# First image's coefficient sums and reconstruction ahead of the odd set's correlation on TensorE

## The chip, the cores and the metric

The kernel runs on one core of one Trainium2 chip. The metric is the device time of one execution in microseconds, the median over several runs. Three runs of the kernel before gave 530.71, 532.79 and 532.80 us.

## What is computed

x is 16 images of 32 channels by 64 by 64, in float32. Each image is normalised per channel, goes through a 3x3 convolution with ternary weights (two weight sets, merged by a gate), and is added to x. The result x1 is normalised again (z) and cut into 256 patches per image, of 32 channels x 4 x 4 = 512 values. Each patch is written by orthogonal matching pursuit as a sum of 5 of 256 normalised dictionary columns, and the sum is added to x1. Cut to what matters:

```python
D = dictionary / (norm(dictionary, axis=0) + 1e-10)       # 512 x 256
G = D.T @ D + 1e-5 * eye(256)
h_bar = (D.T @ X).T                                       # the correlation
h = h_bar
for k in range(1, 6):
    index = argmax(abs(h * ~mask), axis=1)
    ...                                                   # one more row of a Cholesky factor, new x_stack
    h = h_bar - einsum('bk,bkn->bn', x_stack, G[I])
coeffs = zeros((B, 256)).at[bidx[:, None], I].set(x_stack)
X_hat = D @ coeffs.T
x = x + conv(gn(x));  x = x + patches_back(X_hat(gn(x)))
```

## The kernel before, in words

The images are taken in four rounds r = 0 to 3 of four images. A round's patches are two sets: set 0 (the even one) is images 0 and 1 of the round, set 1 (the odd one) images 2 and 3; each set has four tiles of 128 patches. For each set PSUM holds the scores h, one 128x256 block per tile.

Each engine has its order written out by hand; semaphores tie the orders together. `body(r, front, behind)` is one round on one engine. With `front` it also prepares the next round f = r + 1 (statistics of x, convolution, normalisation to z); with `behind` it also finishes images of the round before, b = r - 1. Round 0 has no `behind`, round 3 no `front`.

Matching pursuit (VectorE): per step k and set, `scan` (L992 maxima of |h|, L1005 or L1007 their indices), `select` (the new index; L1049 lets GpSimd gather the Gram rows), `extract` (L1062 picks), `solve` (small solves, whose steps stand between those of the other set's scan). `all_picked(s)` (L983) says at the end of a set's last extraction that h of the set may be overwritten (semaphore `h_read`). In the last step of set 1, `spread(r, 0)` (L1199, L1203) writes four of five terms of image 0's coefficients: five of its eight instructions stand in `select`, the last three after `all_picked(1)`, and then L1208 raises `coef_ready`. ScalarE makes the fifth term (L703, `make_terms`) at the end of the round.

TensorE: `correlate(f, 0)` ends a round's body, `correlate(r, 1)` begins the next; each is 16 products, 32 instructions in the profile (a float32 product shows as two). `correlate(r, 1)` waits for `h_read` of set 1. `coef_transposes(b, m)` transposes and sums the coefficient terms of image m into PSUM: 8 instructions on ScalarE's term, then a wait for `coef_ready`, then 8 on VectorE's. ScalarE's `copy_coef(b, m)` (L689) brings the sum to SBUF, and `reconstruct(b, m)` multiplies it with the atoms (16 instructions). ScalarE's `out_back` (L714) copies the result out; the next image's `coef_transposes` waits for that.

ScalarE, around the start of a round: `scores(f, 0, 0)` for set 0 at the end of the body before; then `x_statistics` of four images (L623), `scores(r, 1, 0)` (L674), `copy_coef(b, 0)`, `root`, `diags(r, 0, 0)` (L683), `out_back(b, 0)`, `norm_x(f, 0)` (L640), `scores(r, 0, 1)`, `copy_coef(b, 1)`, `make_terms` of two images, `norm_x(f, 1)`, `diags(r, 1, 0)`. TensorE's `x_sums(f)` adds the statistics over the channels, VectorE's `variance` (L921 to L935) stands in the scan of set 1, then `root` on ScalarE, then `norm_params` (L941 to L957) on VectorE after the `select` of set 1; it raises `x_params`, for which `norm_x(f, 0)` waits. All matrix products are issued from L391.

Of the kernel before, what the change touches and what calls it, by code (L numbers as in the profile page):

```python
# [32 lines left out]
def build_program(nc, x_in, w_in, b_in, wc_in, bc_in, gate_in, dict_in, out):  # L33
# [25 lines left out]
    with ctx:  # L59
# [81 lines left out]
        def terms_of(r, m):  # L141

            if r < ROUNDS - 1:
                return coef[:, (m + 2) % IMG_R, :, :].rearrange("p (i t) n -> p i t n", i=1)
            first = 2 * ATOMS * sum(ACT_TERMS[r][:m])
            part = spare_z[:, first:first + 2 * ATOMS * ACT_TERMS[r][m]]
            return part.rearrange("p (i t n) -> p i t n", t=2, n=ATOMS)
# [241 lines left out]
        def _(pe):  # L389
            def mm(dst, lhs, rhs, start, stop, skip=False):  # L390
                return nc.tensor.matmul(dst, lhs, rhs, start=start, stop=stop, skip_group_check=skip)  # L391
# [4 lines left out]
            def x_sums(f):  # L396
                pe.wait_ge(x_stats, 2 * IMG_R * (f + 1))
                mm(conv_ps[:, 0, 0:2 * IMG_R], same_channel[:, :], sum_x[:, :, :].rearrange("p a m -> p (a m)"),
                   True, True).then_inc(x_stats_ps, 1)
# [51 lines left out]
            def correlate(f, s):  # L451

                if not (isinstance(f, int) and f == 0):
                    pe.wait_ge(h_read[s], STEPS * f)
                for t in range(TILES):
                    if t % 2 == 0:
                        pe.wait_ge(z_done, IMG_R * f + 2 * s + t // 2 + 1)
                    zt = z[:, 2 * s + t // 2, t % 2 * HALF:(t % 2 + 1) * HALF].rearrange("p (n c) -> p c n", c=PATCH)
                    for c in range(PATCH):
                        last = mm(h[s][:, t, :], zt[:, c, :], d_sb[:, c, :], t % 2 == 0 and c == 0, c == PATCH - 1, True)  # L460
                    if t % 2:
                        last.then_inc(h_ready[s], 1)
# [16 lines left out]
            def coef_transposes(r, m, dst=back_ps[0]):  # L479

                n = IMG_R * r + m
                pe.wait_ge(terms_ready, n + 1)
                if dst is back_ps[0]:
                    pe.wait_ge(y_done, 2 * n + 2)
                of_act = terms_of(r, m)
                for i in range(ACT_TERMS[r][m] + 1):
                    if i == ACT_TERMS[r][m]:
                        pe.wait_ge(coef_ready, n + 1)
                    for k in range(CHUNKS):
                        for t in range(2):  # L490
                            part = coef[:, m, t, :] if i == ACT_TERMS[r][m] else of_act[:, i, t, :]
                            last = mm(dst[:, k, t * P:(t + 1) * P], part[:, k * P:(k + 1) * P], ident[:, :],
                                      i == 0 and k == 0 and t == 0, i == ACT_TERMS[r][m], True)
                last.then_inc(coef_t_ps, 1)
# [10 lines left out]
            def reconstruct(r, m):  # L505

                for half in (1, 0):
                    add_atoms(IMG_R * r + m, half, back_ps[half])
# [30 lines left out]
            def body(r, front, behind):  # L539
                f = r + 1  # L540
                b = r - 1
                idle_bank = conv_ps[:, 1, 0:ATOMS] if behind else back_ps[1][:, 0, :]
                correlate(r, 1)
                if front:
                    x_sums(f)
                if behind:
                    coef_transposes(b, 0)
                    reconstruct(b, 0)
                update(r, 0, 0)
                if behind:  # L550
                    coef_transposes(b, 1)
                    reconstruct(b, 1)
                update(r, 1, 0)
                if not front:
                    pe.wait_ge(x1_done, 2 * IMG_R * ROUNDS)
                if front:
                    conv(f, 0)
                else:
                    keep_busy(idle_bank, 8)
                update(r, 0, 1)  # L560
                if front:
                    conv(f, 1)
                else:
                    keep_busy(idle_bank, 8)
                update(r, 1, 1)
                if front:
                    conv(f, 2)
                else:
                    keep_busy(idle_bank, 8)
                update(r, 0, 2)  # L570
                if front:
                    conv(f, 3)
                else:
                    keep_busy(idle_bank, 6)
                if behind:
                    coef_transposes(b, 2)
                update(r, 1, 2)
                if behind:
                    reconstruct(b, 2)
                else:  # L580
                    keep_busy(idle_bank, 7)
                if front:
                    y_sums(f)
                update(r, 0, 3)
                if behind:
                    coef_transposes(b, 3)
                    reconstruct(b, 3)
                else:
                    keep_busy(idle_bank, 8)
                update(r, 1, 3)  # L590
                if front:
                    correlate(f, 0)
# [9 lines left out]
        def _(act):  # L602
# [83 lines left out]
            def copy_coef(r, m, src=back_ps[0], dst=coef_t):  # L686
                n = IMG_R * r + m
                act.wait_ge(coef_t_ps, n + 1)
                nc.scalar.activation(dst[:, :, :], src[:, :, :], ACT.Copy, scale=-1.0).then_inc(coef_t_done, 1)  # L689
# [62 lines left out]
            def body(r, front, behind):  # L752
                f = r + 1
                b = r - 1
                if front and behind:
                    for m in range(IMG_R):
                        x_statistics(f, m)
                scores(r, 1, 0)
                if behind:
                    copy_coef(b, 0)  # L760
                if front:
                    root(x_var, x_root, 0, f)
                diags(r, 0, 0)
                if behind:
                    out_back(b, 0)
                if front:
                    norm_x(f, 0)
                scores(r, 0, 1)
                if behind:
                    copy_coef(b, 1)  # L770
                    make_terms(b, 2)
                    make_terms(b, 3)
                if front:
                    norm_x(f, 1)
                diags(r, 1, 0)
                if behind:
                    out_back(b, 1)
                scores(r, 1, 1)
                if front:
                    norm_x(f, 2)  # L780
                diags(r, 0, 1)
                if front:
                    out_conv(f, 0)
                scores(r, 0, 2)
                if front:
                    norm_x(f, 3)
                diags(r, 1, 1)
                if front:
                    out_conv(f, 1)
                scores(r, 1, 2)  # L790
                if front:
                    square_sum(f, 0)
                diags(r, 0, 2)
                if front:
                    out_conv(f, 2)
                scores(r, 0, 3)
                if front:
                    square_sum(f, 1)
                diags(r, 1, 2)
                if front:  # L800
                    out_conv(f, 3)
                if behind:
                    copy_coef(b, 2)
                scores(r, 1, 3)
                if front:
                    square_sum(f, 2)
                    square_sum(f, 3)
                diags(r, 0, 3)
                if behind:
                    out_back(b, 2)  # L810
                if front:
                    root(y_var, y_root, 1, f)
                scores(r, 0, 4)
                if behind:
                    copy_coef(b, 3)
                diags(r, 1, 3)
                if front:
                    norm_y(f, 0)
                    norm_y(f, 1)
                if behind:  # L820
                    out_back(b, 3)
                scores(r, 1, 4)
                if front:
                    norm_y(f, 2)
                    norm_y(f, 3)
                    make_terms(r, 0)
                    make_terms(r, 1)
                    scores(f, 0, 0)
# [567 lines left out]
```

## Time and profile before

| | us |
|---|---|
| median of the runs | 532.79 |
| lowest, highest | 530.71, 532.80 |
| the profiled execution, its own time | 535.74 |
| its span, first to last instruction | 533.7 |
| TensorE busy | 429.4 (80%) |
| VectorE busy | 447.4 (84%) |
| ScalarE busy | 317.7 (60%) |
| mean granted TensorE clock | 0.942 of full |

PE is TensorE, PEld its weight loads, DVE VectorE, ACT ScalarE, POOL GpSimd; a q behind the name (DVEq) is the engine's sequencer, which raises semaphores. In a timeline a row gives the start, the time to the end of the last instruction in it, the engine, the line, the operation, the output and the inputs, the count, and in brackets the idle time before with what ended it. Busy time of overlapping instructions is not additive.

### The profile page before, as it was taken

The page shows a single profiled execution, that of the slowest core. Times are in us where ns is not written, and L with a number is a line of the kernel's source. Part 1 is how long each engine was busy: PE and PEld are TensorE (multiplying, and loading weights), DVE is VectorE, ACT ScalarE, POOL GpSimd, SP SyncE. Part 2 cuts the span into 40 slices and gives each one's busy share as a digit, 9 for nine tenths or more (in the row PEclk, how much of TensorE's full clock was granted, in tenths as well). Part 3 has the DMA queues.
Part 4 walks back from the last instruction along what each step waited for, and adds up shares of the span by engine and source line. Part 5 has one row for each costly group of instructions (what it writes and reads, how often), then busy time and mean ns, then how long its engine had stood idle before and what let it go on. Part 6 is the DMA issues. An engine that isn't in the chain of part 4 may idle for free.

```text
span 533.7 us, 7983 instructions
## 1 busy us (share of the span) xinstructions
PE 429.4 (80%) x1948; PEld 324.7 (61%) x1948; DVE 447.4 (84%) x2268; ACT 317.7 (60%) x712; POOL 147.5 (28%) x162
## 2 busy tenths in 40 slices
PE   0089974999885869999894979999958897988685
PEld 0033862556665755557774864568757776867574
DVE  4665668888899959978999889998999999989983
ACT  2535448856558359866697299757740754456340
POOL 3000044433300153532300355443000764430010
PEclk9999997999889887999997899999997999989798
DMA  5999712899300043999510174521400665224256
GB/s 99 176 143 151 139 40 72 139 168 147 68 1 1 9 101 89 161 177 174 119 41 1 29 168 112 132 64 47 83 1 1 158 153 133 68 67 88 47 109 128
DMA packets 110206, 50.76 MB, mean 95 GB/s; under 512 B 103632, under 2 KB 104144, under 8 KB 110160
## 3 DMA queue, kind: packets, MB, share of 16 engines
q1 hardware_dynamic: 99480, 25.60, 29.8%
q0 software_dynamic: 8160, 24.13, 19.6%
q10 hardware_dynamic: 2520, 0.53, 0.5%
q8 instruction: 16, 0.26, 0.2%
q14 instruction: 30, 0.25, 0.2%
HBM read 34.24 MB, written 8.65 MB: 80 GB/s over the span
## 4 chain that ended last, share of the span: by engine, by line
PE 50%; DVE 29%; ACT 8%; issue 6%; SPq 3%; another core or an unknown queue 1%; DMA 1%; DVEq 0%; ACTq 0%
PE h L391 30%; PE conv_ps L391 15%; DVE junk L1062 9%; PE back_ps L391 6%; DVE top L992 3%; SPq L261 3%; DVE top_i L1007 2%; DVE top_i L1005 2%; ACT diag L683 2%; ACT score L674 2%; DVE coef L1203 2%; DVE mask L1089 2%; ACT xb L640 1%; ACT xa L640 1%
## 5 line engine op out<-in xcount | busy, mean ns | idle before, releaser
L363 POOL DMA_INDIRECT rows<-gram,idx_u x128 | 129.1, 1009 | 329.3 <-DVEq L1049 299.2
L391 PE MATMUL h<-rows,diag 128*128 128x256 f32 x640 | 152.3, 395 | 26.0 <-ACT diag L683 22.0
L391 PEld LDWEIGHTS h<-rows,diag 128*128 128x128 f32 x640 | 123.9, 197 | 54.9 <-issue 37.5
L1062 DVE SCALAR_TENSOR_TENSOR junk<-mask,rows 128x256 bf16<-128x256 bf16 x320 | 119.1, 417 | 0.0
L683 ACT ACTIVATE diag<-ident,dx 128x128 f32<-128x128 f32 x320 | 96.8, 388 | 34.8 <-DVEq L1156 33.0
L674 ACT ACTIVATE score<-h 128x512 f32<-128x512 f32 x80 | 47.0, 596 | 97.4 <-PE h L391 85.6
L992 DVE MAX8 top<-score 128x8 f32<-128x256 f32 x160 | 65.1, 418 | 34.5 <-ACT score L674 30.4
L391 PE MATMUL h<-d_sb,z 128*128 128x256 f32 x256 | 68.2, 431 | 23.7 <-DVEq L983 23.7
L391 PEld LDWEIGHTS h<-d_sb,z 128*128 128x128 f32 x256 | 63.5, 329 | 28.7 <-DVEq L983 25.4
L391 PE MATMUL conv_ps<-xa,w_taps 128*64 128x512 f32 x128 | 62.6, 612 | 4.0 <-DVEq L1267 4.0
L391 PE MATMUL conv_ps<-xb,w_taps 128*64 128x512 f32 x128 | 62.6, 612 | 0.0
L391 PE MATMUL back_ps<-coef_t,d_t 128*128 128x256 f32 x224 | 54.1, 397 | 8.9 <-ACT coef_t L689 8.2
L391 PEld LDWEIGHTS back_ps<-coef_t,d_t 128*128 128x128 f32 x224 | 43.3, 197 | 16.9 <-ACT coef_t L689 8.2
L1005 DVE FIND_INDEX8 top_i<-top,h 128x8 uint32<-128x256 f32 x128 | 52.1, 423 | 0.0
L1203 DVE SCALAR_TENSOR_TENSOR coef<-mask,x_last,coef 128x256 f32<-128x256 bf16 x92 | 40.3, 476 | 0.0
L714 ACT ACTIVATE y<-back_ps 128x512 f32<-128x512 f32 x28 | 29.2, 1110 | 11.8 <-PE back_ps L391 7.8
L391 PEld LDWEIGHTS conv_ps<-xa,w_taps 128*64 128x64 f32 x128 | 16.5, 138 | 31.2 <-issue 27.1
L391 PE MATMUL conv_ps<-xa,w_mid 128*64 128x512 f32 x64 | 32.8, 593 | 0.0
L391 PE MATMUL conv_ps<-xb,w_mid 128*64 128x512 f32 x64 | 32.7, 592 | 0.0
L1089 DVE TENSOR_SCALAR mask<-iota_short,idx_u 128x256 bf16<-128x256 bf16 x128 | 28.7, 286 | 3.6 <-DVE idx_u L1044 0.5
L623 ACT ACTIVATE z<-xa 128x1088 bf16<-128x1088 f32 x23 | 25.2, 1099 | 9.5 <-DMA xa<-in_x 9.5
L652 ACT ACTIVATE x<-conv_ps,gn 128x512 f32<-128x512 f32 x32 | 21.5, 674 | 13.7 <-PE conv_ps L391 13.7
(156 smaller groups left out, 569.2 us busy)
## 6 DMA issues: line engine op xcount, KB each, us to landing
xa<-in_x SPq DMA_DIRECT2D x64, 128.0 KB
out<-x SPq DMA_DIRECT2D x60, 128.0 KB, 2.7
x<-y POOLq DMA_DIRECT2D x14, 512.0 KB
xb<-in_x SPq DMA_DIRECT2D x48, 128.0 KB, 4.9
rows<-gram,idx_u POOLq DMA_INDIRECT x128
xb<-in_x SPq DMA_DIRECT2D x16, 120.0 KB, 5.3
d_sb<-in_L_conv_dictionary SPq DMA_DIRECT2D x4, 128.0 KB, 3.9
out<-x ACTq DMA_DIRECT2D x4, 128.0 KB
```

The costliest lines, as they stand in the source:

```text
L363: pool.indirect_dma_start(out=rows[s][:, k, t, :], out_offset=None, in_=gram_dram[:, :], in_offset=bass.IndirectOffsetOnAxis(ap=idx_u[s][: ...
L391: return nc.tensor.matmul(dst, lhs, rhs, start=start, stop=stop, skip_group_check=skip)
L623: nc.scalar.activation(unread[:, n % 3], xa[:, m, :, 1:W + 1], func, accum_out=sum_x[:, i, m:m + 1]).then_inc(x_stats, 1)
L652: nc.scalar.activation(image_of(x1, n)[:, b * HALF:(b + 1) * HALF], conv_ps[:, b, :], ACT.Identity, bias=gn[:, 0, 10, m:m + 1], accum_out= ...
L674: nc.scalar.activation(score[s][:, 2 * b:2 * b + 2, :], h[s][:, 2 * b:2 * b + 2, :], ACT.Abs).then_inc(score_ready[s], 1)
L683: last = nc.scalar.activation(diag[s][:, t, j, :], ident[:, :], ACT.Copy, scale=dx[s][:, k, t, j:j + 1])
L714: nc.scalar.activation(dst[:, 2 * half:2 * half + 2, :], src[half][:, :, :], ACT.Copy).then_inc(y_done, 1)
L992: c = step(v.max(out=top[s][:, t, 0:16:2], in_=score[s][:, t, :]))
L1005: step(v.max_index(out=top_i[s][:, t, :], in_max=top[s][:, t, 0:8], in_values=h[s][:, t, :]))
L1062: c = step(v.scalar_tensor_tensor(out=place, in0=mask_of(r, s, k, t), scalar=1.0, in1=source, op0=ALU.mult, op1=ALU.mult, accum_out=dst))
L1089: marked.append(step(v.tensor_scalar(mask_of(r, s, k, t), iota_short[:, :], idx_u[s][:, k, t:t + 1], None, ALU.is_equal)))
L1203: added.append(step(v.scalar_tensor_tensor(out=coef[:, m, t, :], in0=mask_of(r, s, j, tile), scalar=x, in1=coef[:, m, t, :], op0=ALU.mult, ...
```

## The change

Two moves, in every round that has `behind` (1, 2 and 3). On TensorE the transposes and the reconstruction of image 0 of the round before now stand ahead of `correlate(r, 1)` and `x_sums(f)`, not behind them. On ScalarE the copy between these two products now stands ahead of the statistics of x and of the odd set's scores. No instruction is added or taken away.

```diff
@@ -540,12 +540,12 @@        (block.tensor, body)
                 idle_bank = conv_ps[:, 1, 0:ATOMS] if behind else back_ps[1][:, 0, :]
-                correlate(r, 1)
-                if front:
-                    x_sums(f)
                 if behind:
                     coef_transposes(b, 0)
                     reconstruct(b, 0)
+                correlate(r, 1)
+                if front:
+                    x_sums(f)
                 update(r, 0, 0)
@@ -752,12 +752,12 @@        (block.scalar, body)
+                if behind:
+                    copy_coef(b, 0)
                 if front and behind:
                     for m in range(IMG_R):
                         x_statistics(f, m)
                 scores(r, 1, 0)
-                if behind:
-                    copy_coef(b, 0)
                 if front:
                     root(x_var, x_root, 0, f)
```

## Rows read from the trace of the kernel before

**Rows 1.** The page: the engines' shares of the chain that ended last.

```profile
PE 50%; DVE 29%; ACT 8%; issue 6%; SPq 3%; another core or an unknown queue 1%; DMA 1%; DVEq 0%; ACTq 0%
```

**Rows 2.** Chain of waits, start of round 2 and its middle: start us, us, what.

```profile
291.82 0.03 DVEq L983
...
291.90 10.51 PE h L391 x32
...
302.53 1.90 PE back_ps L391 x16
...
304.45 0.61 ACT coef_t L689
...
305.10 3.73 PE back_ps L391 x16
...
318.94 1.97 PE h L391 x8
...
361.99 0.61 ACT score L674
```

**Rows 3.** Waits of the whole span: engine, line, releaser, total us, times, longest.

```profile
PE h L391 <- DVEq L983: 23.7, 5, 7.4
```

**Rows 4.** Timeline of VectorE, start of round 2: last of image 0's coefficient instructions.

```profile
293.03 0.45 DVE L1203 SCALAR_TENSOR_TENSOR coef<-mask,x_last,coef 128x256 f32<-128x256 bf16 x1
```

**Rows 5.** Timeline of TensorE: `correlate(1, 0)`, at full clock.

```profile
159.97 7.63 PE L391 MATMUL h<-d_sb,z 128*128 128x256 f32 x32
```

**Rows 6.** Granted clock by windows: window, length, busy of five engines, PEclk, DMA.

```profile
168.00:175.00 7.00, 0.01 (x1) 0.01 (x1) 6.88 (x42) 7.00 (x14) 0.00 (x0) 0.77 0.00 0
...
288.00:292.00 4.00, 0.10 (x1) 0.10 (x1) 3.85 (x25) 4.00 (x9) 0.00 (x0) 0.50 0.00 0
...
296.00:299.00 3.00, 3.00 (x11) 2.56 (x10) 2.75 (x8) 0.28 (x1) 0.00 (x0) 0.65 0.00 0
...
312.00:314.00 2.00, 0.33 (x3) 0.14 (x2) 0.85 (x5) 2.00 (x6) 1.70 (x3) 1.00 0.60 140
```

**Rows 7.** Timeline of TensorE, round 1: second image's transposes and reconstruction, at half clock.

```profile
196.64 3.75 PE L391 MATMUL back_ps<-ident,coef 128*128 128x128 f32 x16 [3.51 <-ACT y L714]
201.08 6.11 PE L391 MATMUL back_ps<-coef_t,d_t 128*128 128x256 f32 x16 [0.69 <-ACT coef_t L689]
```

**Rows 8.** Timeline of ScalarE, start of round 2: last statistics, normalisation, diagonals.

```profile
293.06 1.09 ACT L623 ACTIVATE z<-xa 128x1088 bf16<-128x1088 f32 x1
...
309.76 1.15 ACT L640 ACTIVATE xa<-xa,gn 128x960 f32<-128x960 f32 x1
...
318.39 1.28 ACT L683 ACTIVATE diag<-ident,dx 128x128 f32<-128x128 f32 x4
```

**Rows 9.** Timeline of VectorE, round 2: odd set's scan, variance, parameters.

```profile
301.39 0.43 DVE L992 MAX8 top<-score 128x8 f32<-128x256 f32 x1
...
304.22 0.20 DVE L935 TENSOR_SCALAR gn<-gn 128x4 f32<-128x4 f32 x1
...
309.07 0.15 DVE L957 SCALAR_TENSOR_TENSOR gn<-gn 128x4 f32<-128x4 f32 x1
```

**Rows 10.** Timeline of ScalarE, round 1: first image's copy out, then the normalisation.

```profile
190.36 1.13 ACT L714 ACTIVATE y<-back_ps 128x512 f32<-128x512 f32 x1 [2.12 <-PE back_ps L391]
195.43 1.07 ACT L714 ACTIVATE y<-back_ps 128x512 f32<-128x512 f32 x1 [3.94 <-remote]
196.29 1.15 ACT L640 ACTIVATE xa<-xa,gn 128x960 f32<-128x960 f32 x1
```

**Rows 11.** Timeline of TensorE, then VectorE, start of round 3.

```profile
402.76 9.77 PE L391 MATMUL h<-d_sb,z 128*128 128x256 f32 x32 [7.02 <-DVEq L983]
...
416.96 2.46 DVE L1203 SCALAR_TENSOR_TENSOR coef<-mask,x_last,coef 128x256 f32<-128x256 bf16 x6
420.32 0.43 DVE L992 MAX8 top<-score 128x8 f32<-128x256 f32 x1 [0.90 <-ACT score L674]
```

**Rows 12.** Chain of waits in round 3: its last VectorE piece of that stretch.

```profile
448.09 0.47 DVE top_i L1005 x2
```

More of the change, by code:

```diff
@@ L542, in body @@
                 idle_bank = conv_ps[:, 1, 0:ATOMS] if behind else back_ps[1][:, 0, :]
+                if behind:
+                    coef_transposes(b, 0)
+                    reconstruct(b, 0)
                 correlate(r, 1)
@@ L545, in body @@
                     x_sums(f)
-                if behind:
-                    coef_transposes(b, 0)
-                    reconstruct(b, 0)
                 update(r, 0, 0)
@@ L754, in body @@
                 b = r - 1
+                if behind:
+                    copy_coef(b, 0)
                 if front and behind:
@@ L758, in body @@
                 scores(r, 1, 0)
-                if behind:
-                    copy_coef(b, 0)
                 if front:
```

## The prediction

> **What bounds the kernel now.** I read the page's chain first: half of it is TensorE and 29% VectorE [rows 1], so neither engine alone is the bound; they hand the work to each other. Then the chain in order of time at the three round starts with something behind them, where the diff acts. Round 2 is typical [rows 2]: VectorE's last extraction of set 1 releases h at 291.85, TensorE runs `correlate(2, 1)` from 291.90, the sums of x, the transposes, the copy (0.61) and the reconstruction to 308.83. From 318.94 to 361.99 the chain's pieces (nine, two of them shown) are TensorE's without a gap, so what is late at 318.94 stays late. Third, the waits: TensorE stood idle 23.7 us over five waits for L983, up to 7.4 each [rows 3]. That is the hole into which the change puts work. The question is whether that work is ready while the hole is open.
>
> **Is the moved work ready?** The transposes need ScalarE's term and VectorE's four. The latter are complete only when L1208 raises `coef_ready`, and in program order three of the eight instructions of `spread` come after the release of h. In the trace the last of them runs 293.03 to 293.48 [rows 4]; `coef_ready` comes at about 293.5, that is 1.65 us after the release at 291.85 [rows 2]. So only the first 8 of 16 transposing instructions can use the hole; half of 1.90 us, 0.95. The rest starts when h has been free for 1.65 us already, and `correlate(r, 1)` now stands behind it.
>
> **TensorE, start of `correlate(r, 1)`.** New delay against the release of h: 1.65 (wait for `coef_ready`) + 0.95 (second half of the transposes, half of 1.90) + 0.67 (the copy with its two hand-overs, from 304.43 to 305.10) + 3.73 (reconstruction), all from [rows 2, 4]: 7.0 us. The copy in the middle can start at once, since ScalarE is idle there once the statistics are put behind it.
>
> **The clock.** The granted clock falls to half in the hole (0.77 over 168 to 175, 0.50 over 288 to 292) and is back at full only some way into the work (0.65 over 296 to 299) [rows 6]. `correlate(1, 0)` at full clock took 7.63 us [rows 5]; `correlate(r, 1)` took 10.51 in round 2 [rows 2] and 9.77 in round 3 [rows 11], so the cold start costs 2.9 and 2.1 (1.7 in round 1, where it took 9.4 by the same view). After the change the cold start falls on the transposes, a wait for the copy and the reconstruction. The nearest rows are those of round 1 after another idle stretch: 3.75 and 6.11 us [rows 7] where 1.90 and 3.73 are normal, a cost of 4.2 for the whole, or 0.9 + 2.4 = 3.3 for the part that would count here. The first 8 transposes may keep the clock up, and the cost could be nothing. I take 3.2, which is 1.0 more than the mean of before (2.2), with bounds of 2.2 less and 2.0 more.
>
> In a sentence by itself: the Trainium skill, page TensorE: Matmul & The Clock Gate, section What's actually happening, says that the default state is throttled and that activity releases it; by that rule work put into the hole would shorten the cold part, and the sum would be lower by up to 2.2 per round. The trace has the half clock in this hole, but no row with 1 us of work in the middle of it.
>
> **What follows from x_sums (rounds 1 and 2).** Let X be the end of `x_sums`, 302.53 in round 2. It moves by 7.0 + 1.0 = 8.0. Behind X: the variance on VectorE is over at 304.42 (X + 1.9) and the last step of the parameters at 309.22 (X + 6.7) [rows 9], with the odd set's scan and `select` between them, which also trail `correlate(r, 1)`. `norm_x(2+1, 0)` began at 309.76, X + 7.2, since the copy out of image 0 had to end first [rows 8]; then come `scores(2, 0, 1)`, the second image's copy, `norm_x` of the next image and `diags(2, 1, 0)` at 318.39, and TensorE's `update` at 318.94 [rows 2, 8]. After the change the reconstruction is long done, so the copy out follows the diagonals at once and ends about X + 5.5 (variance 1.9, diagonals 1.28 [rows 8], two copies of 1.13 [rows 10]): `x_params` is last, at about X + 6.8. It gains 0.4 on before. Round 2 therefore ends 8.0 - 0.4 = 7.6 later.
>
> New holes also open on TensorE: behind X nothing is left until `diags(r, 0, 0)`, some 3 us, and again about 3.8 us between the second image's transposes (X + 5.5 to 7.5) and its copy (X + 11.3). In round 2 of before the clock stayed up through a shorter hole (1.00 over 312 to 314, with 0.33 of work) [rows 6]. A fall like that of [rows 7] would cost 2.4 on the reconstruction and some on the convolution. 0 to 4; I take 1.0.
>
> **Round 1** has a peculiarity: the second copy out waited 3.94 us for nothing that the profile can name, and `norm_x` began at 196.29, or X + 11.8 (X = 184.5) [rows 10]. Part of that stall becomes cover. If the stall stays at that instruction, the copies are at X + 3.3 and X + 8.3, `norm_x` at X + 9.2: a gain of 2.6 on before, and a bit more since [rows 7] came out cold behind it (reconstruction end X + 22.7 before, about X + 19 after: up to 3.5). If the stall disappears, 5.0. I take 3.3: 8.0 - 3.3 = 4.7.
>
> **Round 3** has no x to prepare. VectorE ended its `spread` at 419.42 and waited 0.90 for the scores of the even set [rows 11]. The odd set's scan and the `spread` behind it trail `correlate(3, 1)`; the even set's scores are now ready in their shadow. VectorE is the late one: 8.0 - 0.9 = 7.1. From there VectorE carries most of the chain, up to 448.56 [rows 12], so it stays.
>
> **ScalarE's move.** Before, the eight statistics (1.09 each) ended at 294.15 [rows 8], within the wait for `correlate`. Now they wait for the copy, to about 295.2, and take 8.9 us, to 304.1. The odd set's first scores come at about 305 and `x_sums` at about 310, so this costs nothing; the cover is 1 us for the scores and 6 for the sums. Without it, the statistics would delay the odd set's scan one for one. SyncE's and GpSimd's orders are untouched; the gather of the odd set's rows starts 8 us later but its last row is due only at X + 16, and the gather itself begins near X + 3.7 and needs about 7: no cost.
>
> **The sum.** 4.7 + 7.6 + 1.0 + 7.1 = 20.4 us. The profiled execution took 535.74 with a span of 533.7; it would take 556.1. The median of before is 532.79, which gives 553.2 us; I say 553.
>
> **Rivals.** (a) Slower as above, for all three rounds: 0.80. Its own range: per round 5.8 to 10 for X instead of 8.0. Low end: round 1 5.8 - 5.0 = 0.8, round 2 5.4, round 3 4.9, sum 11. High end: 10 - 2.6, 9.6 + 4, 9.1, sum 30. Both ends at once in all rounds are unlikely; 543 to 562.
> (b) The clock stays up because the array works in the hole: the term of 3.2 falls to 0 to 1. Then X moves by 7.0 - 2.2 = 4.8 to 5.8, and the total is 1.5 + 4.4 + 3.9 = 10 to 13, or 543 to 546. For it: the hole is cut by 1 us of work. Against: the clock had fallen in both holes of [rows 6] after work that was dense to their start, and 7 us of idle are still left. Chance 0.11.
> (c) Hidden: `correlate(r, 1)` isn't what ends last. VectorE began the odd set's scan at 301.39 [rows 9] without a wait and met X only 1 us later, so that set has about 1 us of slack, not 8; the chain would have to recover 7 us somewhere. 531 to 536, chance 0.04.
> (d) Faster, the other side: the wait for the copy out of image 0 ahead of `norm_x` is what matters, as the chain of round 2 names it, and the work of the block (1.90 + 0.7 + 3.73 = 6.3) leaves the path into the hole of 7. That needs `coef_ready` 6.3 - 1.65, some 4.7 us or more, before the release of h; it decides at the point where `coef_ready` precedes the release. Then up to 6.3 per round are gained, 19 in all: 514. The trace has it 1.65 behind the release [rows 2, 4], and the order of VectorE isn't changed. Chance 0.02.
> (e) Slower by more than (a): the unnamed stall of ScalarE or the cold convolution comes up in more rounds, 4 us each: 562 to 570, chance 0.03.
>
> **How the numbers follow.** The time is that of (a), 553. The range of 543 to 562 takes in (a) but its extremes, and (b). By 0.5% (2.7 us, about what a measurement of this kernel can tell from no change): faster 0.02, the same 0.04, slower 0.94.
>
> **What the profile of the changed kernel would show.** Right: in each of rounds 1 to 3, 8 transposes right behind `correlate(f, 0)`, an idle stretch that now ends with L1208 and not with L983, a reconstruction, and `correlate(r, 1)` beginning about 7 to 9 us after the release of h; the odd set's scan waiting for scores on VectorE for some 8 us; the copy out no longer ahead of `norm_x` in the chain, `x_params` in its place. Wrong: if `correlate(r, 1)` starts late and the first `update` of set 1 doesn't, I misread what is last; if it starts less than 6 us late, the clock term is wrong; if the hole ends before L983, the reading of `coef_ready` is.

## The result: the changed kernel is slower

The changed kernel takes 553.45 us (median; 551.40 to 557.56) beside 531.75 us for the kernel before in the same runs: a ratio of 1.0425, interval 1.0349 to 1.0501. The forecast was 553.0 us, 543 to 562, slower. Ratios, here and below, leave out runs that were slower than the others at a lower clock, so a ratio can differ a little from that of two medians.

The profiled execution took 554.57 us, its span is 552.6 (533.7 before). TensorE's busy time went from 429.4 to 437.8 us and its mean granted clock from 0.942 to 0.925. The page of the changed kernel, part 1 and the chain by engine (to set beside the table and [rows 1]):

```profile
PE 437.8 (79%) x1948; PEld 331.6 (60%) x1948; DVE 447.6 (81%) x2268; ACT 317.0 (57%) x712; POOL 146.7 (27%) x162
...
PE 45%; DVE 34%; ACT 9%; issue 6%; SPq 3%; another core or an unknown queue 1%; DMA 1%; DVEq 0%; ACTq 0%
```

The waits of the changed kernel, whole span, as in [rows 3]:

```profile
DVE top L992 <- ACT score L674: 45.0, 26, 6.1
...
PE back_ps L391 <- DVEq L1208: 23.7, 3, 8.1
...
PE h L391 <- DVEq L983: 2.3, 2, 1.2
```

The hole is still there, three times up to 8.1 us. It now ends with `coef_ready` (L1208), not with the release of h (L983). VectorE waits 45.0 us for scores (L992); in the kernel before:

```profile
DVE top L992 <- ACT score L674: 30.4, 22, 6.4
```

The chain of waits at the start of round 2, changed kernel (start us, us, what), beside [rows 2]:

```profile
295.80 0.02 DVEq L983
...
297.10 0.37 DVE coef L1203
...
297.58 2.09 PE back_ps L391 x8
...
299.69 0.61 ACT coef_t L689
...
300.34 6.68 PE back_ps L391 x16
307.02 7.48 PE h L391 x32
...
314.52 0.61 ACT score L674
...
317.14 3.39 PE h L391 x8
...
325.86 5.41 PE back_ps L391 x16
331.27 1.73 PE h L391 x8
```

h is free at 295.82 and `correlate(2, 1)` begins at 307.02, 11.2 us later; in the kernel before it began 0.05 us after the release. 1.76 us pass until the transposes go on, 2.09 + 0.67 + 6.68 us are the second half of the transposes, the copy and the reconstruction, and all of it is on the chain. Here is the clock in this stretch (window, its length, busy of five engines, PEclk, DMA), as in [rows 6]:

```profile
289.00:297.00 8.00, 0.75 (x7) 0.56 (x6) 7.85 (x45) 0.50 (x1) 0.00 (x0) 0.73 0.00 0
297.00:303.00 6.00, 4.74 (x14) 3.97 (x15) 5.50 (x18) 3.31 (x6) 0.00 (x0) 0.50 0.00 0
303.00:307.00 4.00, 4.00 (x12) 3.24 (x11) 2.18 (x12) 4.00 (x9) 1.16 (x2) 0.58 0.00 0
```

The transposes in the hole did not hold the clock; the reconstruction runs at half of it (1.2 GHz) for the most part, and `correlate` gets the full one (7.48 us).

ScalarE and VectorE behind it, round 2 of the changed kernel, timelines (to set beside [rows 8] and [rows 9]):

```profile
314.64 0.17 DVE L921 TENSOR_SCALAR gn<-conv_ps 128x8 f32<-128x8 f32 x1 [2.39 <-PE conv_ps L391]
...
321.19 0.15 DVE L957 SCALAR_TENSOR_TENSOR gn<-gn 128x4 f32<-128x4 f32 x1
```

```profile
307.83 1.10 ACT L623 ACTIVATE z<-xa 128x1088 bf16<-128x1088 f32 x1
...
317.78 1.98 ACT L714 ACTIVATE y<-back_ps 128x512 f32<-128x512 f32 x2
321.44 1.19 ACT L640 ACTIVATE xa<-xa,gn 128x960 f32<-128x960 f32 x1 [1.68 <-DVEq L961]
```

`norm_x` now waits 1.68 us for L961, which raises `x_params`; the copy out (L714) was over before. The statistics end at 308.93 and `x_sums` comes at 314.3: their cover held.

How much each round costs can be read from one marker, the step L1183 of the odd set's last solve, right behind the release of h. The timelines of VectorE, kernel before, then changed kernel:

```profile
175.03 0.24 DVE L1183 TENSOR_REDUCE n_inv<-prod 128x20 f32<-128x80 f32 x1
...
291.93 0.24 DVE L1183 TENSOR_REDUCE n_inv<-prod 128x20 f32<-128x80 f32 x1
...
402.80 0.24 DVE L1183 TENSOR_REDUCE n_inv<-prod 128x20 f32<-128x80 f32 x1
```

```profile
176.77 0.24 DVE L1183 TENSOR_REDUCE n_inv<-prod 128x20 f32<-128x80 f32 x1
...
295.91 0.24 DVE L1183 TENSOR_REDUCE n_inv<-prod 128x20 f32<-128x80 f32 x1
...
414.89 0.23 DVE L1183 TENSOR_REDUCE n_inv<-prod 128x20 f32<-128x80 f32 x1
```

| | before | changed | difference |
|---|---|---|---|
| up to round 1 (nothing changed) | 175.03 | 176.77 | 1.7 |
| round 1 | 116.90 | 119.14 | 2.2 |
| round 2 | 110.87 | 118.98 | 8.1 |
| round 3 and the end of the span | 130.90 | 137.71 | 6.8 |

The 1.7 us of round 0 is no effect of the change, since nothing differs there. ScalarE has stalls of some 3 us with no releaser that the profile knows (marked "remote"), up to three of them in a profile, and they fall differently from one profile to the next. The changed kernel's had two of them in round 0:

```profile
102.02 0.60 ACT L674 ACTIVATE score<-h 128x512 f32<-128x512 f32 x1 [2.88 <-remote]
...
123.12 0.60 ACT L674 ACTIVATE score<-h 128x512 f32<-128x512 f32 x1 [3.11 <-remote]
```

That of the kernel before had one there. In three later profiles without any in that stretch (half_ahead_2, only_r1, only_r2), where round 0 is the same, the marker stands at 171.10 to 171.86.

### The profile page after: what moved, and what is told of

The parts are those of the page before. It is cut to its first block, busy times and chain, and to the rows that moved or that the text cites. A ratio compares the mean times of both kernels' runs of the same rounds, so it can differ in the third digit from the quotient of the medians.

```text
span 552.6 us, 7983 instructions
## 1 busy us (share of the span) xinstructions
PE 437.8 (79%) x1948; PEld 331.6 (60%) x1948; DVE 447.6 (81%) x2268; ACT 317.0 (57%) x712; POOL 146.7 (27%) x162
## 3 DMA queue, kind: packets, MB, share of 16 engines
q0 software_dynamic: 8160, 24.13, 18.6%
## 4 chain that ended last, share of the span: by engine, by line
PE 45%; DVE 34%; ACT 9%; issue 6%; SPq 3%; another core or an unknown queue 1%; DMA 1%; DVEq 0%; ACTq 0%
PE h L391 25%; PE conv_ps L391 13%; DVE junk L1062 9%; PE back_ps L391 7%; DVE top L992 4%; DVE top_i L1005 3%; DVE coef L1203 3%; SPq L261 3%; ACT diag L683 2%; DVE top_i L1007 2%; ACT score L674 2%; DVE mask L1089 2%; ACT xb L640 2%; DVE coef L1199 1%
## 5 line engine op out<-in xcount | busy, mean ns | idle before, releaser
L391 PE MATMUL h<-rows,diag 128*128 128x256 f32 x640 | 156.9, 404 | 34.4 <-ACT diag L683 29.6
L391 PEld LDWEIGHTS h<-rows,diag 128*128 128x128 f32 x640 | 126.9, 202 | 64.5 <-issue 46.5
L992 DVE MAX8 top<-score 128x8 f32<-128x256 f32 x160 | 65.1, 418 | 47.1 <-ACT score L674 45.0
L391 PE MATMUL back_ps<-coef_t,d_t 128*128 128x256 f32 x224 | 60.7, 432 | 11.6 <-ACT coef_t L689 10.8
L391 PE MATMUL h<-d_sb,z 128*128 128x256 f32 x256 | 61.6, 400 | 2.3 <-DVEq L983 2.3
L391 PEld LDWEIGHTS h<-d_sb,z 128*128 128x128 f32 x256 | 60.3, 328 | 3.7 <-DVEq L983 3.1
L391 PEld LDWEIGHTS back_ps<-coef_t,d_t 128*128 128x128 f32 x224 | 48.0, 219 | 21.8 <-ACT coef_t L689 11.1
L391 PE MATMUL back_ps<-ident,coef 128*128 128x128 f32 x192 | 28.4, 306 | 24.5 <-DVEq L1208 23.7
L391 PEld LDWEIGHTS back_ps<-ident,coef 128*128 128x128 f32 x192 | 27.2, 218 | 27.6 <-DVEq L1208 24.3
```

The source lines that it names most:

```text
L992: c = step(v.max(out=top[s][:, t, 0:16:2], in_=score[s][:, t, :]))
```

## The experiments

All times are medians; a ratio is against runs of the kernel before on the same chip.

**1. Only the transposes ahead (recon_behind).** Against the changed kernel:

```diff
                 if behind:
                     coef_transposes(b, 0)
-                    reconstruct(b, 0)
                 correlate(r, 1)
                 if front:
                     x_sums(f)
+                if behind:
+                    reconstruct(b, 0)
```

> TensorE: the first image's transposes ahead of correlate(r, 1), its reconstruction behind x_sums; ScalarE as in the changed kernel. Theory (everything of the block that stands behind coef_ready delays correlate(r, 1)): only 1.65 us of waiting and some 1 us of transposes are left of the 8 us, so correlate starts about 2.7 us behind the release of h in place of 8 to 11, and the time is 4 to 6 us over the kernel before. Rival (ScalarE's move costs: statistics and odd scores held up behind the copy): it keeps the full 20 us, since the copy stands ahead of the statistics here too.

540.86 us against 532.72, ratio 1.0167 (1.0109 to 1.0224): 8.1 us over the kernel before by the medians, 5.8 to 11.9 by the interval. The theory said 4 to 6, so it was most likely too low, and the 20 of the rival are out. More than half of the loss goes with the reconstruction. What the sum missed shows in TensorE's timeline of round 2 (the lines of this kernel stand one lower):

```profile
290.46 2.08 PE L391 MATMUL back_ps<-ident,coef 128*128 128x128 f32 x8 [7.83 <-DVEq L1209]
292.33 9.36 PE L391 MATMUL h<-d_sb,z 128*128 128x256 f32 x32
301.96 0.39 PE L391 MATMUL conv_ps<-sum_x,same_channel 128*128 128x8 f32 x2 [0.28 <-ACT z L624]
...
313.93 6.73 PE L391 MATMUL back_ps<-coef_t,d_t 128*128 128x256 f32 x16 [3.92 <-ACT coef_t L690]
```

`x_sums` waits 0.28 us for the statistics that were put behind the copy (0.70 in round 1): with `correlate` this early their cover is gone. And 3.92 us of idle ahead of the second image's reconstruction let the clock fall: 6.73 us where the kernel before took 3.72 in that round.

**2. Only the work that is ready put into the hole (half_ahead).** The kernel before, with the 8 transposes of ScalarE's term ahead:

```diff
+                if behind:
+                    coef_transposes(b, 0, parts=(0,))
                 correlate(r, 1)
                 if front:
                     x_sums(f)
                 if behind:
-                    coef_transposes(b, 0)
+                    coef_transposes(b, 0, parts=(1,))
                     reconstruct(b, 0)
```

> The kernel before, with only the 8 transposing instructions on ScalarE's term (ready in the hole) ahead of correlate(r, 1); ScalarE's order as before. Theory: x_sums does not move, the reconstruction ends 0.95 us earlier, of which 0.4 to 0.9 per round counts: 0 to 2 us faster, not clear of noise. Rival (the array kept busy in the hole holds its clock): correlate at 7.6 to 8 us in place of 9.4 to 10.5, 5 to 7 us faster.

529.56 us against 532.72, ratio 0.9951 (0.9915 to 0.9987). The correlations that follow took 9.32, 9.65 and 9.24 us, where the rival said 7.6 to 8: the clock was still down at their start, and the rival falls. The same kernel once more (half_ahead_2):

> half_ahead once more, the same kernel, since its first result (0.995, from 0.992 to 0.999) is close to no change. Theory: a small gain, 1 to 3 us. Rival: none, within 0.2% of before.

524.95 us against 525.12, ratio 0.9981 (0.9960 to 1.0002). So the gain is some 0 to 3 us, and by the second set of runs alone it can't be told from none.

**3. The statistics ahead of the copy (stats_first).** Against the changed kernel, ScalarE:

```diff
-                if behind:
-                    copy_coef(b, 0)
                 if front and behind:
                     for m in range(IMG_R):
                         x_statistics(f, m)
+                if behind:
+                    copy_coef(b, 0)
                 scores(r, 1, 0)
```

> The changed kernel with ScalarE's eight statistics ahead of the first image's copy (TensorE as changed). Theory: the statistics had 6 us of cover behind the copy, so nothing changes: 551 to 556 us. Rival (ScalarE's move costs): clearly faster than the changed kernel, 535 to 545.

552.02 us against 532.72, ratio 1.0350 (1.0278 to 1.0422). The changed kernel's 1.0425 (1.0349 to 1.0501) lies just above this interval, and the two intervals overlap over most of their length: a part of some us can't be ruled out by the times. The traces show none: from marker to marker, rounds 1 and 2 took 118.73 and 118.82 us here, 119.14 and 118.98 in the changed kernel. The 535 to 545 of the rival are out, so the loss goes with TensorE's move.

**4. The coefficients ready in time (early_coef).** The changed kernel, and on VectorE:

```diff
+                    if k == STEPS - 1:
+                        run(rows_of)
                     if not front and k == STEPS - 1:
-                        run(rows_of)
                         run(spread(r, 1))
```

> The changed kernel with one change on VectorE: the last three of the eight coefficient instructions of the round's image 0 stand ahead of the last extraction of set 1, so coef_ready comes some 8 us before the release of h, not 1.65 behind it; h comes free 1.4 us later. Theory: the block goes into the hole, correlate(r, 1) starts at the release (L983) again and is at least partly warm: 526 to 534 us, 20 us under the changed kernel. Rival (the block ahead of correlate costs by its length or by a cold clock whatever it waits for): 545 or more.

532.89 us against 532.72, ratio 1.0009 (0.9972 to 1.0047): the whole loss is gone. TensorE's timeline, round 2:

```profile
280.01 1.95 PE L391 MATMUL back_ps<-ident,coef 128*128 128x128 f32 x16
282.65 3.72 PE L391 MATMUL back_ps<-coef_t,d_t 128*128 128x256 f32 x16 [0.69 <-ACT coef_t L689]
288.62 7.84 PE L391 MATMUL h<-d_sb,z 128*128 128x256 f32 x32 [2.25 <-DVEq L983]
...
300.39 0.89 PE L391 MATMUL h<-rows,diag 128*128 128x256 f32 x2 [3.81 <-DMA rows<-gram,idx_u]
```

The block fits into the hole, 2.25 us of it are left, and `correlate` runs at nearly full speed in this round (7.84 against 10.51 in [rows 2]; 9.37 and 9.36 in rounds 1 and 3). But the kernel isn't faster than the one before. The next thing on TensorE, `update(2, 0, 0)`, now waits 3.81 us for the gathered rows, which the block used to cover; that wait isn't what holds the round, though. The chain of waits, round 2 of early_coef, doesn't pass through it:

```profile
293.59 1.42 DVE top L992 x4
...
299.28 0.18 DVE gn L935
...
304.11 0.03 ACT xa L640
...
313.51 0.30 ACT diag L683
...
313.95 1.97 PE h L391 x8
```

It runs over the scans and the variance on VectorE to `norm_x` on ScalarE, which begins right behind the last step of x's parameters; VectorE's timeline:

```profile
303.87 0.15 DVE L957 SCALAR_TENSOR_TENSOR gn<-gn 128x4 f32<-128x4 f32 x1
```

Counted from the release of h (288.56), `norm_x` begins after 15.6 us (17.9 in the kernel before) and `update(2, 1, 0)` after 25.4 (27.1). So 1.7 us are gained there, not the length of the block, and h comes free 1.4 us later: from marker to marker round 2 took 110.60 us beside 110.87.

**5. The same on VectorE, order as before (early_coef_old_order).** The diff of experiment 4 on the kernel before.

> The order of the kernel before on TensorE and ScalarE, with VectorE's three coefficient instructions ahead of the last extraction. Theory: the release of h is 1.4 us later in each round and nothing uses the early coefficients: 3 to 5 us over the kernel before, so that the changed order, once its inputs are ready, is worth 3 to 4 us of gain (early_coef was level with before). Rival (the place of these instructions costs nothing, and early_coef's level result says that the order is worth nothing even with its inputs ready): within 1.5 us of the kernel before.

533.62 us against 530.52, ratio 1.0058 (1.0018 to 1.0097), 3.1 us over. The later release costs about what was said. The changed order with its inputs ready (experiment 4, 1.0009) would give about that much back, but the difference of the two ratios is 0.0049, or 2.6 us, with an uncertainty as large, so this gain isn't shown.

**6. Filling the next wait too (early_all).** early_coef, and

```diff
@@ TensorE
+                if behind:
+                    coef_transposes(b, 1)
                 update(r, 0, 0)
                 if behind:
-                    coef_transposes(b, 1)
                     reconstruct(b, 1)
@@ ScalarE
+                if behind:
+                    out_back(b, 0)
                 scores(r, 1, 0)
                 if front:
                     root(x_var, x_root, 0, f)
                 diags(r, 0, 0)
                 if behind:
-                    out_back(b, 0)
+                    copy_coef(b, 1)
                 if front:
                     norm_x(f, 0)
                 scores(r, 0, 1)
                 if behind:
-                    copy_coef(b, 1)
                     make_terms(b, 2)
```

> early_coef, plus: the first image's copy out right behind the statistics (ahead of the odd scores), the second image's transposes ahead of update(r, 0, 0), its copy right behind diags(r, 0, 0). They fill the stretch of TensorE that waits for the gathered rows or the diagonals, and the hole ahead of the second reconstruction. Theory (early_coef was held by that wait, the last row comes 8 us behind the index, and by a cold second reconstruction): 524 to 530 us. Rival (the gathered rows and x's parameters set the pace whatever TensorE does): 531 to 534.

528.65 us against 530.52, ratio 0.9966 (0.9930 to 1.0002). It lies inside what the theory said in us, but against its own runs of before it is only 1.9 us and not clear of none. TensorE's timeline, round 2:

```profile
292.74 2.03 PE L391 MATMUL back_ps<-ident,coef 128*128 128x128 f32 x16
295.49 0.67 PE L391 MATMUL h<-rows,diag 128*128 128x256 f32 x2 [0.72 <-DMA rows<-gram,idx_u]
...
308.06 3.75 PE L391 MATMUL h<-rows,diag 128*128 128x256 f32 x8 [4.98 <-ACT diag L684]
```

The first wait for rows is down to 0.72 us, and the odd set's update waits 4.98 us for its diagonals (1.08 in early_coef). The chain of this round again passes through x's parameters and `norm_x`; in round 3, where there is no x, it passes through the gather:

```profile
408.06 2.82 DMA rows<-gram,idx_u
```

So the mechanism that the rival named, x's parameters and the rows, is what the chain shows, though its 531 to 534 us were not met.

**7. One round at a time (only_r1, only_r2, only_r3).** The kernel before with both moves in one round only:

```diff
+                ahead = r == 1          # 2, 3
+                if ahead:
+                    coef_transposes(b, 0)
+                    reconstruct(b, 0)
                 correlate(r, 1)
                 if front:
                     x_sums(f)
-                if behind:
+                if behind and not ahead:
                     coef_transposes(b, 0)
                     reconstruct(b, 0)
```

and ScalarE's copy likewise.

> The change in round 1 alone. In the traces so far ScalarE's unnamed stall of some 3 us is at another instruction in every kernel (twice, once or not at all in a profile), so the 3.94 us that the trace of before had at round 1's copy out belongs to no place. Theory (round 1 is a round like the others; 8 to 9 us behind the release and little given back): 6 to 8 us over the kernel before. Rival (as I predicted, the stall stands in that place and the change hides it): 3 to 5 us over.

> The change in round 2 alone. Theory (delay of x_sums 8.0 us, almost nothing given back since x_params then sets norm_x, and a cold second reconstruction): 7 to 9 us over the kernel before, the largest of the three rounds. Rival (the three rounds aren't independent, and alone one costs less): under 5 us over.

> The change in round 3 alone, where no x is prepared and VectorE carries the chain. Theory: correlate(3, 1) ends 7.4 us later, 0.9 was idle, 6 to 7.5 us over the kernel before. Rival (round 3 takes back part of it, since the statistics and x_sums aren't there): under 4 us over.

| change in | time | before | ratio (interval) | over before, us |
|---|---|---|---|---|
| round 1 | 535.33 | 530.52 | 1.0096 (1.0056 to 1.0137) | 5.1 (3.0 to 7.3) |
| round 2 | 532.83 | 525.12 | 1.0140 (1.0115 to 1.0166) | 7.4 (6.0 to 8.7) |
| round 3 | 537.64 | 530.52 | 1.0137 (1.0058 to 1.0216) | 7.3 (3.1 to 11.5) |

(The last column is the ratio less 1, times the time of before.) The three add up to 19.8 us; the whole change costs 22.6 (18.6 to 26.6). The rounds are independent within what the intervals can tell. For round 1 the interval holds both the theory and its rival. The traces say more. Without a stall at its first image's copy out, round 1 in the old order took 110.07 us from marker to marker (only_r2); with the block ahead it took 118.38 (only_r1), 118.73 (stats_first) and 119.14 (changed kernel), 8.3 to 9.1 more. With that stall the old order took 116.90 (kernel before, 3.94 us of stall) and 115.85 (only_r3, 4.62).

## Why the prediction was right, point by point

- **Is the work ready?** Right, and this is the cause. `coef_ready` comes after the release; TensorE continues 1.76 us behind it in round 2 (1.65 forecast for `coef_ready`). Experiment 4 moves only that event and takes the loss away.
- **Delay of correlate(r, 1).** 11.2 us behind the release in round 2. X (the end of `x_sums`) moved from 10.7 us behind the release to 18.8 (314.60 less 295.82): 8.1, where 8.0 stood. In round 1 it moved by 9.1, in round 3 (end of `correlate`) by 7.4.
- **The clock.** 3.2 us stood for the cold block. Measured against the full-speed times of 1.05 and 3.72 it is 1.03 + 2.96 = 4.0 in round 2, 3.8 in round 1 and 2.5 in round 3 (reconstructions of 6.68, 6.52 and 5.24, transposes 2.08): 3.4 on average. Over the cold start that `correlate` had before in the same round (2.9, 1.7, 2.1) that is 1.1, 2.1 and 0.4, where 1.0 stood. 1.05 us of work in the hole did not keep the clock in any of the three rounds, nor in half_ahead. The Trainium skill (TensorE: Matmul & The Clock Gate, What's actually happening) has activity releasing the throttle; these runs bear that out for the work behind the hole (0.50, then the full clock). The 1.05 us at the hole's start did not help.
- **Behind x_sums, round 2.** Right: `x_params` sets `norm_x`, at X + 6.8 (321.44) where X + 6.8 stood. The new hole ahead of the second reconstruction was 3.56 us long and let the clock fall, as feared: 5.41 in place of 3.72. The first new hole, 2.53 us ahead of the even set's update, left its mark too: 3.39 us in place of 1.89. What each of the two holes cost the round by itself was not measured. (From 318.94 to 361.99 the chain of before has ten pieces of TensorE, where the prediction counts nine; nothing hangs on that.) Round 2 cost 8.1 in the trace, 7.4 alone, 8.6 in the sum.
- **Round 1.** 4.7 stood, 8.0 less 3.3 given back, and what was given back hung on a 3.94 us stall in the one trace of before; 2.2 in the trace, 5.1 (3.0 to 7.3) alone. The stall at round 1's copy out is in two more profiles of the old order in that round (4.62 in only_r3, 1.83 in early_coef_old_order), in none of the three others (half_ahead, half_ahead_2, only_r2), and in none of the five in which the block stands ahead in round 1. So it was wrong of me to say, ahead of only_r1, that it belongs to no place; but it is no fixed part of the kernel before either. Against a round without it the change costs 8.3 to 9.1 us, as the delay of X says, and almost nothing is given back. That 4.7 came near the 5.1 is in part luck: it took one execution for the average, and how often the stall comes was not counted. What it is stays open.
- **Round 3.** 7.1 stood; 6.8 in the trace, 7.3 alone.
- **ScalarE's move at no cost.** Right for the changed kernel as far as experiment 3 can tell, and by the row of the statistics only because `correlate` is so late. In experiment 1, where it is earlier, `x_sums` waits 0.3 to 0.7 us for them.
- **The sum.** 20.4 us against 21.7 by the medians. The rivals fall: (e) was not reached, the highest run being 557.56; (b), the clock held, by the rows of 0.50; (c), hidden, by the result. The faster one (d) named its own condition, `coef_ready` ahead of the release by 4.7 us or more; experiment 4 makes it true and gains 20 us on the changed kernel, but not the 19 on the kernel before that (d) named. That term was mis-sized: it took the whole block off the path, though the prediction's own row had x's parameters at X + 6.8, only 0.4 us ahead of the copy out that they replace. In early_coef `norm_x` indeed begins 7.5 us behind X (304.11 less 296.57, the end of `x_sums`), where it was 7.2; what moved is X, by the warmer `correlate`. It also left out the 1.4 us by which h comes free later.

## What to carry to other kernels

An idle stretch of an engine is room only for work whose inputs are there when it begins; look for the semaphore that the moved work waits for and set its time beside the end of the stretch, because what stands behind that wait in the engine's order waits with it, as `correlate` did here. Here an event 1.7 us too late turned a block of 6.3 us, which would have fitted into the hole, into a delay of 7 to 9 us. When the inputs are brought forward, ask which other chain ends at nearly the same time as the work that leaves the path: here it was x's parameters, and with them hardly anything was gained. A wait that appears on the freed engine (here 3.81 us for gathered rows) need not be what holds the round.

## What I had not expected of the hardware

- 1.05 us of matmuls at the start of an idle stretch of 9 us did not keep the clock: 0.73 over 289 to 297, 0.50 over 297 to 303, as the stretch without them had ended at 0.50 [rows 6].
- One gap of 2.25 us ahead of `correlate` left its speed nearly whole in round 2 of early_coef (7.84 us), but in rounds 1 and 3 the same gap gave 9.37 and 9.36 us. The same idle time at the same place costs 0.2 or 1.7 us.
- ScalarE's unnamed stalls: up to three of some 3 us in a profile, 11.2 us in one (half_ahead, with two short ones), none in four (half_ahead_2, only_r1, only_r2, early_all). I did not find what releases them.
